# A two-block model kernel on one core: the product of W_out and the scaled W_in on rounded parts and residues, and the second group's normalisation moved on VectorE

## What is computed

```python
xn = _layernorm(x, axis=-1)
s = _L0_attn_ref(xn, W_in, W_out, A_theta, B_real, B_imag, C_real, C_imag, norm_w)
g = _silu(_L0_ffn_ref(xn, W1, W2, W3))
x = x + s * g
```

```python
xi = (x @ W_in.T).reshape(b, l, NC, D)[..., None]
bxr = B_real * xi
bxi = B_imag * xi
nr = ct * rs - st * is_ + bxr
ni = st * rs + ct * is_ + bxi
y = jnp.sum(C_real * nr - C_imag * ni, axis=-1)
out = y.reshape(b, l, NC * D) @ W_out.T
return (x + _rmsnorm(out, norm_w), nr, ni)
```

## Time and profile before

| | us |
|---|---|
| median of 3 runs | 355.48 |
| lowest, highest | 355.45, 355.92 |
| the profiled execution | 355.35 |
| its span, first to last instruction | 353.6 |
| PE busy | 348.7 (99%) |
| DVE busy | 252.4 (71%) |
| ACT busy | 168.3 (48%) |
| POOL busy | 106.3 (30%) |

### The profile page before, as it was taken

The page is one execution under the profiler, slowest core; times in us unless marked ns, Lnnn a source line. Parts: engine busy times, 40 slices in busy tenths (PEclk is TensorE's granted clock), DMA queues, the critical chain, the costliest instruction groups (busy, mean ns, idle before and its releaser), DMA issues.

```text
span 353.6 us, 4944 instructions
## 1 busy us (share of the span) xinstructions
PE 348.7 (99%) x1761; PEld 296.0 (84%) x1761; DVE 252.4 (71%) x498; ACT 168.3 (48%) x332; POOL 106.3 (30%) x122
## 2 busy tenths in 40 slices
PE   8999999999999999999999999999999999999996
PEld 5888888888888888888978878888888888888896
DVE  5679964995499666966588876787657886467645
ACT  2865442447254724454465644654346544464510
POOL 2164410466136933663025030150300703004000
PEclk9999999999999999999999999999999999999999
DMA  7989579205160403140341401626014251064001
GB/s 236 262 189 231 150 111 124 67 33 133 46 137 12 121 0 119 34 119 0 105 144 43 128 2 59 182 43 195 3 57 146 67 174 36 2 191 133 3 0 61
DMA packets 69664, 34.44 MB, mean 97 GB/s; under 512 B 40708, under 2 KB 69640, under 8 KB 69640
## 3 DMA queue, kind: packets, MB, share of 16 engines
q1 hardware_dynamic: 69224, 33.80, 37.9%
q10 hardware_dynamic: 416, 0.33, 0.3%
HBM read 21.99 MB, written 12.12 MB: 96 GB/s over the span
## 4 chain that ended last, share of the span: by engine, by line
PE 95%; DVE 2%; ACT 2%; issue 0%; ACTq 0%
PE GU L358 20%; PE GU L359 20%; PE GU L360 20%; PE O L358 8%; PE O L359 8%; PE O L360 8%; PE GU L525 1%; PE O L426 1%; PE O L507 1%; PE O L508 1%; PE O L506 1%; PE T L365 1%; PE GU L365 1%; PE T L360 1%; PE T L359 1%; PE T L358 1%
## 5 line engine op out<-in xcount | busy, mean ns | idle before, releaser
L722 ACT ACTIVATE hf<-GU 128x512 f32<-128x512 f32 x64 | 38.2, 599 | 80.4 <-DVE hid L842 64.3
L998 DVE TENSOR_TENSOR hf<-hf,GU 128x512 f32<-128x512 f32 x64 | 43.5, 680 | 28.4 <-PE GU L360 22.5
L842 DVE TENSOR_TENSOR hid<-hf,hid 128x512 fp32r<-128x512 f32 x64 | 50.6, 791 | 0.3
L358 PE MATMUL GU<-XT,W1T 128*128 128x512 f32 x128 | 50.6, 396 | 0.1
L360 PE MATMUL GU<-XT,W1T 128*128 128x512 f32 x128 | 49.9, 390 | 0.0
L358 PE MATMUL GU<-XT,W3T 128*128 128x512 f32 x128 | 49.8, 389 | 0.0
L359 PE MATMUL GU<-XT,W1T 128*128 128x512 f32 x128 | 49.8, 389 | 0.0
L360 PE MATMUL GU<-XT,W3T 128*128 128x512 f32 x128 | 49.8, 389 | 0.0
L359 PE MATMUL GU<-XT,W3T 128*128 128x512 f32 x128 | 49.8, 389 | 0.0
L358 PE MATMUL O<-hid,W2hi 128*128 128x512 f32 x112 | 44.0, 393 | 0.0
L359 PE MATMUL O<-hid,W2hi 128*128 128x512 f32 x112 | 43.7, 390 | 0.0
(11 more groups left out here) (204 smaller groups left out, 715.7 us busy)
## 6 DMA issues: line engine op xcount, KB each, us to landing
swap_rows<-GX SPq DMA_DIRECT2D x7, 512.0 KB, 3.3
sT<-swap_rows SPq DMA_DIRECT2D x28, 128.0 KB, 2.7
swap_gate<-GX SPq DMA_DIRECT2D x7, 512.0 KB, 2.9
sT<-swap_gate SPq DMA_DIRECT2D x28, 128.0 KB, 2.7
stage<-in_L_ffn_W SPq DMA_DIRECT2D x12, 256.0 KB, 4.2
swap_p<-PX SPq DMA_DIRECT2D x4, 640.0 KB, 3.3
PL<-swap_p SPq DMA_DIRECT2D x16, 160.0 KB, 3.2
stage<-in_L_ffn_W SPq DMA_DIRECT2D x32, 64.0 KB, 2.6
```

The costliest lines, as they stand in the source:

```text
L358: pe.matmul(o, lhs(0), rhs(0), start=start, stop=False)
L722: act.activation(hf[:, c % 2, :], GU[:, c % 2, 0, :], ACT.Silu).then_inc(silu_done, 1)
L842: dve.tensor_tensor(dst, src, hi_part.bitcast(F32), ALU.subtract).then_inc(done, 1)
L998: dve.tensor_tensor(hf[:, c % 2, :], hf[:, c % 2, :], GU[:, c % 2, 1, :], ALU.mult).then_inc(mul_done, 1)
```

## The change

M is no longer a float32 product. ScalarE writes the scaled W_in as a rounded part, `winH`, and VectorE its residue, `winL` (`win_residue`, over the place of win); W_out is turned in place as before, then ScalarE writes `woutH` and VectorE `woutL`, in halves. `small_m` waits for `win_lo` and `wout_lo` and issues `mm3`: 24 matmuls of 256 columns instead of eight in float32. VectorE's work on group 1 stands earlier: statistics behind chunk 1, normalisation behind the vector k, the turn behind chunk 3. GpSimd's `rstd_of(1)` stands behind the first pair of butterflies.

```diff
--- before.py
+++ after.py
@@ -110,8 +110,13 @@
         W1T0 = sb("W1T0", [P, 2, KC, H], F32R)
         W3T0 = sb("W3T0", [P, 2, KC, H], F32R)
         with ExitStack() as early:
-            win = sb("win", [P, MC, D], F32, early)
-            woutT = sb("woutT", [P, MC, D], F32, early)
+            with ExitStack() as sooner:
+                win = sb("win", [P, MC, D], F32, sooner)
+                woutT = sb("woutT", [P, MC, D], F32, sooner)
+            winL = sb("winL", [P, MC, D], F32R, early)
+            woutL = sb("woutL", [P, MC, D], F32R, early)
+            winH = sb("winH", [P, MC, D], F32R, early)
+            woutH = sb("woutH", [P, MC, D], F32R, early)
             wo = sb("wo", [P, KC, D], F32, early)
             wqkvT = sb("wqkvT", [P, 3, KC, D], F32, early)
             ssm = sb("ssm", [P, 5, MC, DS], F32, early)
@@ -186,7 +191,8 @@
         w_turned, wx_hi, wx_lo, natx_hi, natx_ready = sem("w_turned"), sem("wx_hi"), sem("wx_lo"), sem("natx_hi"), sem("natx_ready")
         kv_loaded = sem("kv_loaded")
         wout_loaded, wqkv_loaded, wo_loaded = sem("wout_loaded"), sem("wqkv_loaded"), sem("wo_loaded")
-        wout_turned, wqkv_turned, win_scaled = sem("wout_turned"), sem("wqkv_turned"), sem("win_scaled")
+        wout_turned, wqkv_turned = sem("wout_turned"), sem("wqkv_turned")
+        win_hi, win_lo, wout_hi, wout_lo = sem("win_hi"), sem("win_lo"), sem("wout_hi"), sem("wout_lo")
         xnext_loaded = sem("xnext_loaded")
         w2_loaded, w2_turned = sem("w2_loaded"), sem("w2_turned")
 
@@ -416,15 +422,15 @@
                 pe.transpose(O[:, 0, 0:2 * KC], gbrow[:, :], ident[0:2 * KC, 0:2 * KC]).then_inc(gb_tr, 1)
 
             def small_m():
-                pe.wait_ge(win_scaled, MC)
-                pe.wait_ge(wout_turned, MC // 2)
+                pe.wait_ge(win_lo, MC)
+                pe.wait_ge(wout_lo, MC // 2)
                 pe.wait_ge(w_lo, 2 * PAIRS)
                 pe.wait_ge(u_ready, PAIRS)
                 pe.wait_ge(gb_ready, 1)
                 for k in range(KC):
                     for m in range(MC):
-                        last = pe.matmul(O[:, 0, k * D:(k + 1) * D], win[:, m, k * P:(k + 1) * P], woutT[:, m, :],
-                                         start=(m == 0), stop=(m == MC - 1))
+                        last = mm3(O[:, 0, k * D:(k + 1) * D], lambda a: (winH, winL)[a][:, m, k * P:(k + 1) * P],
+                                   lambda a: (woutH, woutL)[a][:, m, :], m == 0, m == MC - 1)
                 last.then_inc(sm_mm, 1)
 
             def small_av():
@@ -754,9 +760,11 @@
                 nat_hi(3, w2nat)
                 act.wait_ge(kvec_ready, 1)
                 for m in range(MC):
-                    act.activation(win[:, m, :], win[:, m, :], ACT.Identity, scale=kvec[:, m:m + 1]).then_inc(win_scaled, 1)
+                    act.activation(winH[:, m, :], win[:, m, :], ACT.Identity, scale=kvec[:, m:m + 1]).then_inc(win_hi, 1)
                 chunk(0, 4, True)
                 chunk(0, 5, True)
+                for h in (0, 1):
+                    hi(woutH[:, 2 * h:2 * h + 2, :], woutT[:, 2 * h:2 * h + 2, :], wout_turned, h + 1, wout_hi)
                 pair_u(0, 3, 3)
                 hi(gb[:, :, :].rearrange("p g k -> p (g k)"), O[:, 0, 0:2 * KC], gb_tr, 1, gb_ready)
                 chunk(0, 6, True)
@@ -875,6 +883,12 @@
                 dve.wait_ge(kstep, 4)
                 dve.tensor_reduce(kvec[:, :], kprod[:, 0, :, :], AX_X, ALU.add).then_inc(kvec_ready, 1)
 
+            def win_residue():
+
+                for m in range(MC):
+                    dve.wait_ge(win_hi, m + 1)
+                    dve.scalar_tensor_tensor(winL[:, m, :], win[:, m, :], kvec[:, m:m + 1], winH[:, m, :].bitcast(F32), ALU.mult, ALU.subtract).then_inc(win_lo, 1)
+
             def small_lo(q):
                 R, bank = ((MR, O[:, 0, :]), (AR, T[:, 0, :]), (VR, T[:, 1, :]))[q]
                 lo(R[:, 1, :, :].rearrange("p k d -> p (k d)"), bank, R[:, 0, :, :].rearrange("p k d -> p (k d)"),
@@ -1083,20 +1097,23 @@
                 pair_lo(0, 1, 1)
                 nat_lo(1, w2nat)
                 chunk(0, 1)
+                dve.wait_ge(xnext_loaded, 16)
+                stats(1, TILES)
                 pair_lo(0, 2, 2)
                 nat_lo(2, w2nat)
                 chunk(0, 2)
                 k_vector()
+                normalise(1, TILES)
                 chunk(0, 3)
-                dve.wait_ge(xnext_loaded, 16)
+                x_turn(1)
                 pair_lo(0, 3, 3)
                 nat_lo(3, w2nat)
-                stats(1, TILES)
                 chunk(0, 4)
-                normalise(1, TILES)
+                win_residue()
                 turn_wout()
                 chunk(0, 5)
-                x_turn(1)
+                for h in (0, 1):
+                    lo(woutL[:, 2 * h:2 * h + 2, :], woutT[:, 2 * h:2 * h + 2, :], woutH[:, 2 * h:2 * h + 2, :], wout_hi, h + 1, wout_lo)
                 chunk(0, 6)
                 turn_wqkv()
                 w2_sums(0)
@@ -1277,10 +1294,10 @@
                     pool.wait_ge(stats_ready, h + 1)
                     pool.tensor_tensor(rstd[:, 2 * h:2 * h + 2], vtmp[:, 2 * h:2 * h + 2], mhalf[:, 2 * h:2 * h + 2], ALU.pow).then_inc(rstd_ready, 1)
                 pair_butterfly(0, 0, 1)
+                rstd_of(1)
                 pair_butterfly(0, 1, 2)
                 quad_butterfly(0, 0, 4)
                 pair_butterfly(0, 2, 3)
-                rstd_of(1)
                 pair_butterfly(0, 3, 4)
                 quad_butterfly(0, 1, 10)
                 last_butterfly(0, 12)
```

## The result

The changed kernel takes 361.62 us, the median of five runs (361.52 to 361.94); the kernel before took 355.65 beside it (five runs, 355.45 to 355.92). The ratio is 1.0165, with a 95% interval of 1.0154 to 1.0175: slower by 6.0 us. The forecast was 360.7, in a range of 357.0 to 363.0. The profiled execution took 361.52, with a span of 359.7 against 353.6.

A forecast was written before the change was run, and what follows sets the result against it. TensorE's own unbroken stream was taken to bound the kernel. VectorE's late operands, net of the product's 0.47 us gain, move the down projection from 47.07 to 52.5: 355.35 + 5.4 = 360.7 us, range 357.0 to 363.0.

The forecast's parts named there:

- the four places named: TensorE waits for VectorE: 0.7 us at chunk 5, 0.8 at the last Hadamard product, 3.3 at the product, 1.2 after the mix.
- The product's gain: At the product of W_in and W_out, 24 matmuls on rounded parts replace float32 ones: 0.47 us saved on TensorE.
- The W2 rounding: ScalarE's rounding of W2, behind GpSimd's last butterfly and sum of halves: starts at 46.4 instead of 40.71.
- the vector k: VectorE's scale vector, four tiny operations taking turns with GpSimd's additions: ready at 26.9 instead of 23.3.
- the bound with a wait before each: At the scale vector, each of four tiny operations waits for GpSimd: vector ready at 27.9.
- W_in's residues: Four added VectorE operations before the product, taken at 1.40 us in all without an accumulator operand.
- The sum without collisions: VectorE's work back to back from 17.79 to the product comes to 17.7 us: last operand ready at 35.5.
- the restart: At the product, after its stall, TensorE needs some 0.25 us to notice the signal and refill the array.
- The rival at +0.9: Nothing collides before the product, only VectorE's added work counts: +0.9 us, 356.3 us; chance 0.12.
- Tiny operations slip through: Scale vector comes at 24.3, only residues collide, product starts at 36.7: +2.9 us, 358.2 us; chance 0.17.
- The clock: The 3.3 us pause before the product cools TensorE, product up to 3 us longer: +1.8, 362.5 us; chance 0.12.
- VectorE keeps up: VectorE's idle time before the product absorbs the added work, W_out's residues ready before 34.4: 354.9 us; chance 0.06.

The follow-up runs named there:

- root_later: Changed kernel with GpSimd's inverse root of group 1 behind the first wide pair of butterflies; 359.25 us, ratio 1.0100 to the kernel before.
- fit: `gaps_tail` with normalisation ahead of W_in's residues, turns of group 1 and attention's weights ahead of chunk 6; 357.7 us, ratio 1.0056 to the kernel before.
- parts_only: Changed kernel with the product on parts kept, VectorE's group 1 work and GpSimd's inverse root put back; 360.53 us, ratio 1.0132 to the kernel before.
- k_first: Changed kernel with the vector k made right behind the statistics, ahead of the third pair's residues; 360.33 us, ratio 1.0130 to the kernel before.
- pair_waits: `root_later` with GpSimd's fourth pair of butterflies held until W_out's residues are made; 361.15 us, ratio 1.0145 to the kernel before.
- the halves: Each against the kernel before: group 1's work and inverse root moved, product float32, 359.1 us; product on rounded parts without those moves, 360.53 us.
- copy_first: Changed kernel with ScalarE's copy of the last Hadamard part ahead of W_out's rounding; 363.15 us, ratio 1.0213 to the kernel before.
- gaps: Changed kernel, W_out turned behind vector k, its residues on GpSimd, statistics and inverse root back, normalisation behind chunk 5; 361.23 us, ratio 1.0158 to the kernel before.
- gaps_tail: `gaps` with the second half of W2's residues behind the residues AR and VR; 361.45 us, ratio 1.0162 to the kernel before.
- norm_late: Kernel before with only group 1's normalisation moved behind chunk 5 and its turn behind chunk 6; 359.3 us, ratio 1.0103.

## Why the prediction was right, and where it was off

**Right in kind.** TensorE's stream was broken at the four places named, by VectorE each time, and nothing behind 53 us gave anything back. The product's gain was 0.49, forecast 0.47. Starts of TensorE, forecast and measured: chunk 5 28.95 and 29.25, product 39.3 and 39.78, down product 52.5 and 53.08. The W2 rounding was put at 46.4 and came at 46.88.

**Off by 0.7 us, in three terms.** The largest is the vector k: I stepped through the turns and let two tiny operations pass between the wide additions, giving 26.9. In the trace each of the four waits for an addition of its own, and k is ready at 27.31; the bound with a wait before each was 27.9. The normalisation behind it starts at 27.22, 0.3 later than forecast. `root_later` is the run that shows it was this collision: without it k is ready at 24.55, and 2.2 us go. The second is W_in's residues, taken at 1.40 for lack of a row and measured at 1.66, or 1.58 as a step (33.89 to 35.47): 0.2 more. The listed form with an operand in the accumulators (1.67) was the better row. These two bring the rounding of W2 to 46.88 instead of 46.4. The third is in the reading, not in the kernel: the times at which TensorE was due, 28.28, 34.55 and 47.07, came from the chain of waits, which lists these matmuls 0.16 later than the timeline (28.12, 34.39, 46.91), while VectorE's times came from the timeline. So every delay in the forecast is too short by 0.16, and the starts compared above look closer than the delays are: 0.58 at the down product, where the delay misses by 6.17 - 5.4 = 0.77.

**The sum without collisions was right, and it is not a case that occurs.** Two kernels, with their collisions taken off, give 35.7 and 35.6 for the forecast's 35.75. That it fits to 0.1 is in part luck: W_in's residues are 0.18 longer, and the restart, taken at 0.25, is 0.10 in the timeline of `root_later` (residue done at 37.37, product at 37.47). And none of the orders tried is free of them. Where one part of VectorE's work was moved out of the way, another met the same additions: the normalisation (1.82, 2.76, 5.98), a residue of hid (1.52), W_in's residues (3.63), W_out's (3.42). The rival at +0.9 had 0.12; the nearest to it are `fit` at +2.0, with another order, and `root_later` at +3.8.

**"Tiny operations slip through" fell** on its condition; its price was low as well. `root_later` has the condition met in fact, and costs 3.8 instead of 2.9, since the copy and the normalisation collide there too.

**The clock** was a chance of 0.12 at +1.8 more. The changed kernel's profiled run has no fall, so the delays listed above owe nothing to it. Its other four runs have a mean clock of 0.995 instead of 0.999 and are 0.1 to 0.4 slower. That is the mean of the profiled run of `root_later`, which shows a fall, so the clock probably fell in them as well, mostly hidden by the wait behind the mix; no trace shows it. Runs of one kernel with and without a fall price it at 0.9 (`parts_only`), 1.5 (`k_first`) and nothing visible (`root_later`), less than my estimate each time: the product lost 2.3 in `parts_only` and `k_first` instead of 3, and the wait behind the mix hid about as much as the 1.2 that I had allowed, or more. Why it falls in some executions and not in others is open. The Trainium skill ("TensorE: Matmul & The Clock Gate", Why this matters for your kernels) warns of idle gaps; the falls behind the pauses of `parts_only` and `pair_waits` agree, the changed kernel's profiled run, at 1.00 behind 3.05 us, does not.

**VectorE keeps up** missed by 5 us. Even with the collisions taken off, VectorE's own work ends over 1 us too late.

What is shown by a run: the place of the inverse root (2.2 us), the halves (3.6 and 5.1), the place of the normalisation (3.6 in the kernel before). That the rest of the 6.0 is VectorE's 2.8 us of added residues and the late copy follows from rows, and wasn't taken apart further: both attempts (`copy_first`, `pair_waits`) moved the loss to the other wait, and a fall of the clock, 1.3 and 1.6 us, makes up most of what they were slower by.

## What to carry to other kernels

Where one engine's stream is unbroken, an edit that saves it 0.5 us and asks 2.8 us of another is decided by that other engine's slack up to the first deadline: sum it, then add a neighbour's whole instruction for every operation beside GpSimd's additions that is of a kind that took turns here, however small it is: two inputs in SBUF, a copy or the normalisation's form. An order that has run without waits has fitted its operations to the pauses of the neighbour; a move that looks free on its own engine has to be checked against what now runs beside it, and against the copies queued behind it on a third. Two instructions on GpSimd, moved behind the next four additions, were worth 2.2 us. A comparison of two kernels that let TensorE pause needs the granted clock of every run beside it: up to 1.6 us between such kernels here was the clock's.

## What the runs showed that I had not expected

- Operations with a single tensor input in SBUF take turns with GpSimd's additions as well: the normalisation, 1.37 for four alone, took up to 5.98; a copy of four columns 0.92 instead of 0.17. The statistics, the transposes and the products with an accumulator bank kept their times beside them (statistics 1.40 and 0.38 in `root_later`, three transposes 1.88 in the changed kernel). The section of the Trainium skill that I had used for two inputs ("SBUF — State Buffer", Who interferes with whom) also names copies and tensor_scalar, the normalisation's kind, among the operations that can take the ports shared with GpSimd. I had passed over that; the trace agrees with it, and my expectations of `gaps` and `root_later` were too low, in part by it.
- The normalisation with constants ran in 0.28 an operation at its shortest, against 0.41 with scalars from SBUF.
- GpSimd's power operation on four columns, 1.02 us long, held up none of the tiny operations beside it; its additions of 0.7 to 1.3 us held up all of them.
- The granted clock fell to 0.50 in eight of the profiled runs. It fell in or soon after waits of 1.7 us (`fit`), 2.1 (`pair_waits`), 2.4 (`root_later`), 3.0 (`k_first`), 3.3 (`parts_only`), 3.7 (`gaps`), 4.2 (`gaps_tail`) and 4.7 (`copy_first`). It kept 1.00 behind waits of 2.1 (`norm_late`) and 3.05 (the changed kernel). So the length of the wait alone does not tell whether it falls.
